# Tiles of four consecutive tokens per partition: a mixer's running sums by neighbour additions and one triangle product, one logit product a batch

## The chip, the cores and the metric

The kernel runs on one NeuronCore of a Trainium2 chip. The metric is the device time of one execution in microseconds (us). Engines are named as in the profile: PE is TensorE (PEld its weight loads), DVE VectorE, ACT ScalarE, POOL GpSimd, SP the engine that issues most DMAs (its queue is SPq).

## The reference, cut to what matters

Two layers on x of 8 batches x 512 tokens x 256 channels. Each layer adds to x a mixer's result times the Silu of a mixture of experts. Around the change, layer 0:

```python
xn = layernorm(x)
# mixer
q, k, v = split(rms_norm(xn) @ w_qkv.T); q = rms_norm(q); k = rms_norm(k)
w = exp(k); kv = w * v
w = cumsum(w, axis=tokens); kv = cumsum(kv, axis=tokens)
y = sigmoid(q) * kv / (w + 1e-06)
u, g = split(y @ w_swiglu.T); s = xn + (u * silu(g)) @ w_out.T
# experts: each of 16 experts takes its 64 best tokens of every batch
logits = silu(xn @ router_w1) @ router_w2
probs = softmax over tokens; weights, indices = top_k(probs, 64)
expert_out = (silu(xe @ w1) * (xe @ w2)) @ w3; f = scatter_add(weights * expert_out)
x = x + s * silu(f)
```

The running sum goes over all 512 tokens of a batch, for 512 channels (w and kv). Layer 1 has softmax attention with 16 heads and 8 experts of which each token takes 2, and a shared expert.

## The kernel before, in words

Everything is float32; the large expert products are split into a high and a low part and done as three products of the faster float32r form (`product3`, L93). A batch of 512 tokens is held as four tiles of 128 tokens: token 128 t + p stands in partition p of tile t (`tiled`, L1935). There are five stages, each a block with one instruction stream per engine and semaphores between them.

1. `layer0_norm` (L108): layernorm of the eight batches, transposition, router hidden layer (L162) and router logits: four small products per batch (L170), each copied by VectorE to `k.logits` (L247). SP loads x two batches ahead, then fills `f` with zeros (L141).
2. `layer0_mix_and_experts` (L261): first the choice of tokens (L708 to L746), for which four transposes (L428) bring the logits to one row per batch and expert; beside it batch 0's qkv products. Then batch 0's sums and divides, two qkv of batch 1, the first expert's input; then the main list.
3. `layer1_prepare` (L779): layernorms, projections and routing logits of layer 1.
4. `layer1_route` (L1097): slots of the chosen tokens.
5. `layer1_attend_and_feed` (L1216): attention beside the experts of layer 1, and the final sum.

**The order in stage 2** is a list written out by the program and walked by every engine. 16 experts have six steps each: ("up", e, 0..3), ("down", e, 0..1). The mixer's steps are ("qkv", n, t), ("sum", n, t), ("turn", n, 0), ("gates", n, 0..1), ("out", n, 0) for batch n and tile t. Before the change one mixer step follows each expert step, in one running list (L306 to L318); so a batch, 12 or 13 mixer steps, takes two experts. A step has its part on each engine:

- up (L406): 12 products of 512 columns into the banks GATE and VALUE, after `h_done` of the step before. ScalarE does the Silu (`expert_gate`, L505), VectorE the product with the value (`hidden`, L699), ScalarE its rounding (`high_h`, L510), VectorE the rest (`low_h`, L704). ScalarE rounds a weight of the next expert (`high_w`, L490) ahead of the Silu in up 1, 2, 3, and VectorE takes its rest (`low_w`, L688) between `hidden` and `low_h`.
- down (L415): 24 products of 256 columns; the first down waits for `h_lo` of each of the four parts. After it stands the transposition of the next expert's input (`transpose_x`, L398), then `high_x` (L499) and `low_x` (L693).
- qkv (L354): products of one tile into the banks QK and V, after `qkv_sb` of the tile before; VectorE copies them (`copy_qkv`, L635), ScalarE takes the sums of squares (`squared`, L461). After the fourth tile GpSimd makes the norm factors (`factors`, L559).
- exponentials (`exps`, L469, eight instructions) and the values (`keys_values`, L644) stand in the first down of an odd expert, and GpSimd's two partial sums (`partial`, L582) too.
- sum (L362): the tile's running sum by a product with an upper triangle of ones (L369) and, from tile 1 on, a product of ones with the sum of the tiles before (L372). VectorE then divides (`divide`, L652: four instructions, one of them a reciprocal of 1.75 us).
- turn (L375), gates (L382), out (L390): y transposed, its high part copied by ScalarE (`copy_y`, L479) and low part by VectorE (`low_y`, L669), the two gate products, `gate` (L485) and `gated` (L674), the last product and `residual` (L680).

Each engine does its parts strictly in the order of the list; an instruction that waits holds up all that stand behind it on its engine.

## Time and profile before

| | us |
|---|---|
| median of three runs | 1772.76 |
| lowest and highest run | 1771.67, 1774.93 |
| the profiled execution's own time | 1770.29 |
| its span, first to last instruction | 1768.3 |
| TensorE, VectorE, ScalarE, GpSimd busy | 1576.7, 1166.1, 918.9, 739.4 |
| mean granted TensorE clock | 0.942 of full |

By stage, read from the timelines: stages 1 and the choice of tokens to 99 us, experts and mixer of layer 0 to 605, the last scatter and the preparation of layer 1 to 772, routing to 802, attention and experts of layer 1 to the end.

How to read it: the profile is one execution. A timeline row is "start us, us, engine line op out<-in (partitions x elements) xcount [idle time before it <- what ended it]". Products overlap by a fraction of their length, so starts are compared, not ends. A granted clock of 1.00 is 2.4 GHz, 0.50 is 1.2 GHz.

### The profile page before, as it was taken

How to read it: one execution, taken by the hardware profiler on the slowest of the kernel's cores; microseconds unless marked ns; L12 is line 12 of the kernel's file. 1: busy time of each engine (PE TensorE's matmuls, PEld its weight loads, DVE VectorE, ACT ScalarE, POOL GpSimd, SP SyncE). 2: the span in 40 equal slices, each digit the busy share in tenths (PEclk: the TensorE clock that was granted, in tenths of full speed). 3: DMA queues.
4: the chain of work that ended last, by engine and by line, in shares of the span. 5: the costliest groups of instructions: out<-in, count | busy, mean ns of one | idle time of the engine just before them, and what ended most of it. 6: DMA issues, size and time to landing. Idle time of an engine off the chain costs nothing.

```text
span 1768.3 us, 27041 instructions
## 1 busy us (share of the span) xinstructions
PE 1576.7 (89%) x9562; PEld 1140.3 (64%) x9562; DVE 1166.1 (66%) x1847; ACT 918.9 (52%) x1426; POOL 739.4 (42%) x664
## 2 busy tenths in 40 slices
PE   6679999999999549954999999999999999999976
PEld 4357767877877435632677777777777777777631
DVE  6747567567557156656766666777777777777647
ACT  2335545545545123311555556777776777676644
POOL 3406335334433255502323223556565555555410
PEclk9899999999999869975999999999999999999975
DMA  6715546445333268845233335767676667666464
GB/s 223 232 37 114 149 96 141 122 99 141 74 90 87 24 214 293 308 161 150 87 107 114 100 124 137 196 159 195 165 188 161 182 165 185 175 176 184 115 187 147
DMA packets 218918, 265.38 MB, mean 150 GB/s; under 512 B 19616, under 2 KB 160416, under 8 KB 218784
## 3 DMA queue, kind: packets, MB, share of 16 engines
q1 hardware_dynamic: 191904, 227.92, 42.6%
q0 software_dynamic: 26880, 35.73, 11.3%
q8 instruction: 77, 1.26, 0.3%
q14 instruction: 57, 0.47, 0.1%
HBM read 174.30 MB, written 88.75 MB: 149 GB/s over the span
## 4 chain that ended last, share of the span: by engine, by line
PE 39%; SPq 4%; DVE 3%; DMA 2%; ACT 1%; issue 1%; POOL 0%; DVEq 0%; ACTq 0%
PE a_hidden_bank L93 16%; PE a_bank L93 8%; PE a_bank L1522 5%; PE a_max_bank L1491 5%; PE a_score_bank L1512 3%; DMA a_ka<-qk 2%; SPq L1314 2%; SPq L1318 2%; PE a_max_bank L1537 1%; PE a_bank L1529 1%; DVE a_w20lo L1828 1%; ACT a_xThi L1670 1%; DVE a_neg_max L1787 1%; DVE a_hT1lo L1818 0%; SPq L1380 0%
## 5 line engine op out<-in xcount | busy, mean ns | idle before, releaser
L1648 ACT ACTIVATE a_prob<-a_score_bank 128x1024 f32<-128x1024 f32 x240 | 246.2, 1026 | 257.1 <-PE a_score_bank L1512 214.9
L1787 DVE TENSOR_REDUCE a_neg_max<-a_max_bank 128x2 f32<-128x1024 f32 x249 | 304.1, 1221 | 91.8 <-PE a_max_bank L1491 86.2
L1444 POOL DMA_INDIRECT fs<-a_y,a_token x80 | 127.1, 1589 | 189.2 <-ACT a_y L1696 164.9
L1491 PE MATMUL a_max_bank<-a_ka,a_qa 48*128 48x512 f32 x498 | 128.0, 511 | 23.4 <-DVE a_neg_max L1787 12.0
L1522 PE MATMUL a_bank<-a_prob,a_va 128*32 128x512 f32 x1024 | 147.2, 650 | 0.5 <-DVE a_ml L1796 0.5
L602 POOL DMA_INDIRECT f<-e_ye,c_slot_row x64 | 100.7, 1573 | 84.6 <-issue 64.6
L1810 DVE SCALAR_TENSOR_TENSOR a_tg<-a_tg,a_hidden_bank 128x512 f32<-128x512 f32 x112 | 76.7, 685 | 82.1 <-ACT a_tg L1658 82.1
L1512 PE MATMUL a_score_bank<-a_qa,a_ka 50*128 50x512 f32 x480 | 100.2, 413 | 5.1 <-DMA a_qa<-a_ml 2.7
L702 DVE TENSOR_TENSOR e_h<-e_bank,e_sge 128x512 f32<-128x512 f32 x64 | 44.3, 691 | 89.2 <-ACT e_sge L508 82.6
L358 PE MATMUL e_bank<-m_wqkv,x_rows 128*128 128x512 f32 (+1 forms) x256 | 91.3, 501 | 8.8 <-DVE e_qkv L642 8.8
L1491 PEld LDWEIGHTS a_max_bank<-a_ka,a_qa 48*128 48x128 f32 x498 | 47.9, 189 | 69.9 <-DVE a_neg_max L1787 23.3
L93 PE MATMUL a_hidden_bank<-a_xThi,a_w31hi 128*128 128x256 f32 x288 | 89.4, 310 | 0.0
L93 PE MATMUL e_bank<-e_w3hi,e_heThi 128*128 128x256 f32 x256 | 80.1, 313 | 8.8 <-DVE e_heTlo L706 8.8
L1658 ACT ACTIVATE a_tg<-a_hidden_bank 128x512 f32<-128x512 f32 x112 | 67.2, 600 | 38.7 <-PE a_hidden_bank L93 37.2
L1814 DVE TENSOR_TENSOR a_h<-a_hidden_bank,a_tg 128x512 f32<-128x512 f32 x112 | 77.5, 692 | 13.8 <-PE a_hidden_bank L93 1.9
L93 PE MATMUL a_hidden_bank<-a_xThi,a_w11hi 128*128 128x256 f32 x288 | 85.2, 296 | 0.0
L93 PE MATMUL a_hidden_bank<-a_xThi,a_w31lo 128*128 128x256 f32 x288 | 82.3, 286 | 0.0
L93 PE MATMUL a_hidden_bank<-a_xTlo,a_w11hi 128*128 128x256 f32 x288 | 82.3, 286 | 0.0
L93 PE MATMUL a_hidden_bank<-a_xTlo,a_w31hi 128*128 128x256 f32 x288 | 82.1, 285 | 0.0
L93 PE MATMUL a_hidden_bank<-a_xThi,a_w11lo 128*128 128x256 f32 x288 | 82.1, 285 | 0.0
L508 ACT ACTIVATE e_sge<-e_bank 128x512 f32<-128x512 f32 x64 | 38.1, 595 | 81.1 <-PE e_bank L93 81.1
L595 POOL DMA_INDIRECT e_xg<-xn,c_slot_row x64 | 70.9, 1108 | 20.7 <-issue 18.6
(352 smaller groups left out, 4782.0 us busy)
## 6 DMA issues: line engine op xcount, KB each, us to landing
a_raw<-in_W SPq DMA_DIRECT2D x120, 512.0 KB
e_raw<-in_w SPq DMA_DIRECT2D x48, 512.0 KB, 3.8
a_qa<-qk SPq DMA_DIRECT2D x192, 64.0 KB
a_ka<-qk SPq DMA_DIRECT2D x192, 64.0 KB
xs<-c_pad SPq DMA_DIRECT2D x20, 516.0 KB
a_xg<-xs SPq DMA_DIRECT2D x20, 516.0 KB, 4.7
qk<-p_hi SPq DMA_DIRECT2D x32, 256.0 KB, 5.8
qk<-p_lo SPq DMA_DIRECT2D x32, 256.0 KB, 5.4
```

Of the source, the lines that this page charges most:

```text
L93: ins = nc.tensor.matmul(out, a[i][x], b[l][y], start=first and n == m == 0, stop=last and n == len(pairs) - 1 and m == 2)
L358: ins = nc.tensor.matmul(bank[:, 0:f1 - f0], m.xnT[:, n, ch, t * P:(t + 1) * P], m.wqkv[:, ch, f0:f1], start=ch == 0, stop=ch == DC - 1)
L595: nc.gpsimd.indirect_dma_start(xg[u][:, t, :], None, xn_rows, bass.IndirectOffsetOnAxis(k.slot_row[:, e, t:t + 1], 0)).then_inc(xg_in[u], 16)
L602: nc.gpsimd.indirect_dma_start(f_rows, bass.IndirectOffsetOnAxis(k.slot_row[:, e, t:t + 1], 0), ye[:, t, :], None, compute_op=ALU.add).the ...
L1444: nc.gpsimd.indirect_dma_start(f_rows, bass.IndirectOffsetOnAxis(token[x % 4][:, t:t + 1], 0), y[:, t, :], None, compute_op=ALU.add).then_ ...
L1491: nc.tensor.matmul(max_bank(g, m)[:, s, :], qa[q][rows, p, t * P:(t + 1) * P], ka[q][rows, p, :], start=True, stop=True).then_inc(p1_ps, 1)
L1512: nc.tensor.matmul(score_bank(g, u)[:, s, :], ka[q][rows, p, j * P:(j + 1) * P], qa[q][rows, p, :], start=True, stop=True).then_inc(s_ps, 1)
L1522: ins = nc.tensor.matmul(OB[rows, :], va[g % NR][:, j, rows], prob[j % 2][:, h_, :], start=j == 0, stop=j == T - 1, tile_position=(0, 32 * ...
L1648: nc.scalar.activation(prob[j % 2][:, 2 * p:2 * p + 2, :], score_bank(g, u)[:], ACT.Exp, scale=float(D) ** -0.5).then_inc(p_done, 1)
L1787: nc.vector.tensor_reduce(neg_max[:, g % 2, :, T * p + t], max_bank(g, m)[:], AX.X, ALU.max, negate=True).then_inc(mx_done, 1)
L1810: nc.vector.scalar_tensor_tensor(tg[:], tg[:], 1.0, GATE[:], ALU.add, ALU.mult).then_inc(act_done, 1)
L1814: nc.vector.tensor_tensor(h[:], VALUE[:], tg[:], ALU.mult).then_inc(h_done, 1)
```

## The change

- A tile is now four consecutive tokens per partition: token 4 p + t stands in partition p of tile t, and a DMA of a batch reads 4 KB in a row. `grouped` keeps the old form for the expert groups of layer 1.
- The running sum within a partition is three additions on GpSimd, tile t-1 onto tile t (`prefix`). One product of a strict triangle with the last tile gives what stands before each partition; `divide` adds it to numerator and denominator.
- The router's logits of all batches are gathered in one bank, one product of 512 columns a batch, with router_w2 set in zeros so that each batch writes its own 16 rows; one copy at the end instead of eight, and no transposes in the choice.
- The order of stage 2 is written per expert: in an even expert a qkv step after each up, in an odd one turn, gates, gates and out. Divides, exponentials, values and additions stand at new places. Batch 0's divides move from before the first expert into it, and batch 1's first two qkv steps as well.
- The zeros of `f` are written in stage 2, x is loaded four batches ahead, norm factors are made per batch.
- In stage 5 the loads of q and k are issued before two weight loads, and ScalarE rounds x before those weights.

The diff, cut to its core:

```diff
@@ layer0_norm, TensorE @@
 def logits(n):
-    for t in range(T):
-        ins = nc.tensor.matmul(B[6 + n % 2][:, t * E0:(t + 1) * E0], hT[:, n % 2, t * P:(t + 1) * P], rw2[:], start=True, stop=True)
+    first = (NB - 1 - n) * E0
+    nc.tensor.matmul(B[6][:], rw2[:, first:first + P], hT[:, n % 2, :], start=n == 0, stop=n == NB - 1).then_inc(lg_ps, 1)
...
+    order = []
+    for e in range(E0):
+        n, steps = e // 2 + 1, [("turn", e // 2, 0), ("gates", e // 2, 0), ("gates", e // 2, 1), ("out", e // 2, 0)]
+        for f in range(FC):
+            order.append(("up", e, f))
+            if e % 2:
+                order.append(steps[f])
+            elif n < NB:
+                order.append(("qkv", n, f))
+        order += [("down", e, 0), ("down", e, 1)]
+    def next_batch(e):
+        return (e + 1) // 2 if e % 2 and e + 1 < E0 else 0
...
-            def sum_(n, t):
...
+            def sum_(n):
+                pe.wait_ge(sums_done, 3 * (n + 1))
+                pe.wait_ge(s0_done, n)
+                nc.tensor.matmul(MIX[0][:], k.strict[:], wkv[:, T - 1, :], start=True, stop=True).then_inc(cum_ps, 1)
...
@@ TensorE, before the list @@
             transpose_x(0)
+            sum_(0)
...
                     down(a, i)
+                    if i == 0 and next_batch(a):
+                        sum_(next_batch(a))
                     if i == 0 and a + 1 < E0:
                         transpose_x(a + 1)
...
@@ ScalarE, the list @@
                     expert_gate(a, i)
                     high_h(a, i)
+                    if i == 0 and next_batch(a):
+                        exps(next_batch(a))
                 elif kind == "down":
-                    if i == 0 and a % 2 and a + 1 < E0:
-                        exps((a + 1) // 2)
...
@@ GpSimd @@
+            def prefix(n):
+                for t in range(1, T):
+                    pool.wait_ge(kv_done, T * n + t + 1)
+                    pool.wait_ge(sums_done, 3 * n + t - 1)
+                    nc.gpsimd.tensor_tensor(wkv[:, t, :], wkv[:, t - 1, :], wkv[:, t, :], ALU.add).then_inc(sums_done, 1)
...
+                elif kind == "up" and i == 1 and next_batch(a):
+                    prefix(next_batch(a))
...
@@ VectorE @@
             def divide(n, t):
+                total = MIX[0]
+                dve.wait_ge(cum_ps, n + 1)
                 dve.wait_ge(exp_done, 2 * T * n + T + t + 1)
+                own.step(nc.vector.scalar_tensor_tensor(den[:, t % 2, :], total[:, 0:D], CUM_EPS, wkv[:, t, 0:D], ALU.add, ALU.add))
+                own.step(nc.vector.tensor_tensor(y[:, t, :], total[:, D:2 * D], wkv[:, t, D:2 * D], ALU.add))
+                own.wait(1)
+                own.step(nc.vector.scalar_tensor_tensor(rec[:, t % 2, :], qkv[:, t, 0:D], 1.0, den[:, t % 2, :], ALU.add, ALU.mult))
                 own.wait()
                 own.step(nc.vector.reciprocal(den[:, t % 2, :], rec[:, t % 2, :]))
                 own.wait()
+                nc.vector.tensor_tensor(y[:, t, :], y[:, t, :], den[:, t % 2, :], ALU.mult).then_inc(y_done, 1)
...
@@ VectorE, the list @@
                     low_h(a, i)
+                    if a == 0:
+                        divide(0, i)
+                    elif a % 2 == 0 and i < 2:
+                        divide(a // 2, 2 + i)
+                    if i == 1 and next_batch(a):
+                        keys_values(next_batch(a))
+                elif kind == "down":
+                    if next_batch(a):
+                        divide(next_batch(a), i)
+                    if i == 0 and a + 1 < E0:
                         low_x(a + 1)
...
@@ layer1_attend_and_feed, SP @@
             load_x(0)
+            load_qk(0)
             load_w(0, 0)
             load_w(1, 0)
-            load_qk(0)
...
@@ layer1_attend_and_feed, ScalarE @@
+            high_x(0)
             high_w(0, 0)
             high_w(1, 0)
-            high_x(0)
...
     def tiled(ap, t=T):
-        return ap.rearrange("(b t p) d -> b p t d", t=t, p=P)
+        return ap.rearrange("(b p t) d -> b p t d", t=t, p=P)
```

## Rows read from the trace of the kernel before

**Rows 1.** Windows: us; busy (count) of PE, PEld, DVE, ACT, POOL; clock; DMA:

```profile
100.00:600.00 500.00, 474.05 (x2310) 369.35 (x2309) 305.68 (x445) 244.79 (x474) 196.72 (x179) 1.00 0.43 102
```

**Rows 2.** TensorE's waits in stage 2: total us, times, longest:

```profile
PE e_bank L93 <- DVE e_h L702: 10.4, 16, 1.4
PE e_bank L93 <- DVE e_heTlo L706: 7.0, 7, 2.1
```

**Rows 3.** TensorE's timeline: the same sum product, five batches apart:

```profile
233.70 1.02 PE L369 MATMUL e_bank<-e_wkv,c_upper 128*128 128x512 f32 x2
...
554.02 1.02 PE L369 MATMUL e_bank<-e_wkv,c_upper 128*128 128x512 f32 x2
```

**Rows 4.** TensorE's timeline through an even expert:

```profile
235.98 0.50 PE L93 MATMUL e_bank<-e_xeThi,e_w10hi 128*128 128x512 f32 x1 [0.41 <-DVE e_h L702]
...
238.83 2.74 PE L358 MATMUL e_bank<-m_wqkv,x_rows 128*128 128x512 f32 x8
241.48 0.50 PE L93 MATMUL e_bank<-e_xeThi,e_w10hi 128*128 128x512 f32 x1
...
248.97 0.39 PE L93 MATMUL e_bank<-e_w3hi,e_heThi 128*128 128x256 f32 x1 [0.83 <-DVE e_heTlo L706]
...
250.87 1.04 PE L403 MATMUL e_bank<-c_ident,e_xg 128*128 128x128 f32 x8
```

**Rows 5.** VectorE's timeline in the same expert:

```profile
232.08 0.42 DVE L657 SCALAR_TENSOR_TENSOR e_den<-e_bank,e_qkv 128x256 f32<-128x256 f32 x1
...
235.24 0.69 DVE L702 TENSOR_TENSOR e_h<-e_bank,e_sge 128x512 f32<-128x512 f32 x1
...
240.74 0.69 DVE L702 TENSOR_TENSOR e_h<-e_bank,e_sge 128x512 f32<-128x512 f32 x1
...
243.08 0.68 DVE L641 COPY e_qkv<-e_bank 128x512 f32<-128x512 f32 x1
...
246.49 0.69 DVE L702 TENSOR_TENSOR e_h<-e_bank,e_sge 128x512 f32<-128x512 f32 x1 [2.40 <-ACT e_sge L508]
```

**Rows 6.** ScalarE's timeline between the last two of rows 5:

```profile
244.13 0.42 ACT L467 ACTIVATE e_squares<-e_qkv 128x256 f32<-128x256 f32 x1 [2.03 <-DVE e_qkv L642]
...
244.94 1.04 ACT L497 ACTIVATE e_w21hi<-e_raw 128x1024 fp32r<-128x1024 f32 x1
```

**Rows 7.** ScalarE's timeline: the exponentials of a batch begin:

```profile
280.09 1.28 ACT L475 ACT_TABLE_LOAD   x1
281.38 1.71 ACT L475 ACTIVATE e_wkv<-e_qkv,e_scale 128x256 f32<-128x256 f32 x4
```

**Rows 8.** ScalarE and VectorE: high and low part of turned y:

```profile
264.63 1.07 ACT L483 ACTIVATE e_yThi<-e_bank 128x512 fp32r<-128x512 f32 x2
...
265.37 1.28 DVE L672 TENSOR_TENSOR e_yTlo<-e_bank,e_yThi 128x512 fp32r<-128x512 f32 x2
```

**Rows 9.** Expert 0's last fetch and first product, expert 15's last result:

```profile
84.59 0.95 POOL L595 DMA_INDIRECT e_xg<-xn,c_slot_row  x1 [0.30 <-issue]
...
99.32 0.47 PE L93 MATMUL e_bank<-e_xeThi,e_w10hi 128*128 128x512 f32 x1
...
604.42 0.84 ACT L521 ACTIVATE e_ye<-e_bank,c_slot_share 128x256 f32<-128x256 f32 x2 [2.04 <-PE e_bank L93]
```

**Rows 10.** GpSimd's timeline: first scatter and last fetch of an expert step:

```profile
226.56 1.62 POOL L602 DMA_INDIRECT f<-e_ye,c_slot_row  x1 [3.53 <-issue]
...
238.18 0.95 POOL L595 DMA_INDIRECT e_xg<-xn,c_slot_row  x1 [0.30 <-issue]
```

**Rows 11.** SP's and TensorE's timelines at the start of stage 5:

```profile
802.72 2.58 SPq L1341 DMA_DIRECT2D a_raw<-in_Ws  x2
...
816.66 0.80 PE L1491 MATMUL a_hidden_bank<-a_ka,a_qa 48*128 48x512 f32 x2 [7.19 <-DMA a_ka<-qk]
```

**Rows 12.** Windows of 2 us before expert 0, columns as in rows 1:

```profile
74.00:76.00 2.00, 0.00 (x0) 0.00 (x0) 1.97 (x6) 0.91 (x4) 0.57 (x3) 0.90 0.63 175
76.00:78.00 2.00, 0.14 (x1) 0.14 (x2) 1.64 (x8) 0.00 (x0) 1.72 (x3) 0.50 1.09 369
...
94.00:96.00 2.00, 0.13 (x2) 0.00 (x0) 1.83 (x3) 0.00 (x0) 0.00 (x0) 1.00 0.09 35
```

More of the change, by code:

```diff
@@ L198, in _ @@
-            own.step(nc.gpsimd.memset(m.half[:], -0.5))
-            own.wait()
+            flat_rstd = rstd[:].rearrange("p b t -> p (b t)")
+            flat_var = mv[:, :, :, 1].rearrange("p b t -> p (b t)")
+            first = Steps(pool, half_set, 2, 0)
+            first.step(nc.gpsimd.memset(m.half[:], -0.5))
+            first.step(nc.gpsimd.memset(rw2[:], 0.0))
+            first.wait()
+            first.end()
             for n in range(NB):
+                own = Steps(pool, r_done, 6, n)
+                now = slice(n * T, (n + 1) * T)
@@ L210, in _ @@
[L210 to L219 removed]
+                pool.wait_ge(rstd_done, n + 1)
@@ L221, in _ @@
+                own.wait()
+                own.step(nc.gpsimd.tensor_tensor(m.r2sq[:, now], m.r2[:, now], m.r2[:, now], ALU.mult))
+                own.step(nc.gpsimd.tensor_scalar(m.r2neg[:, now], m.r2[:, now], -1.0, None, ALU.mult))
+                own.wait()
+                own.end()
         @block.vector
@@ L748, in _ @@
             keys_values(0)
-            for t in range(T):
-                divide(0, t)
-            copy_qkv(1, 0)
             low_x(0)
-            copy_qkv(1, 1)
             for kind, a, i in order:
@@ L756, in _ @@
                     copy_qkv(a, i)
-                elif kind == "sum":
-                    divide(a, i)
                 elif kind == "turn":
```

172 lines of the change are left out of this document (52 added, 120 removed).

## The prediction

> **What bounds the kernel now.** The page's busy times stand first: TensorE leads. That is an average over five stages, and the change touches mostly the second, mixer and experts of layer 0. So next came the table of windows for that stage: of 500 us TensorE is busy 474, VectorE 306, ScalarE 245, at full clock [rows 1]. TensorE's waits in it are small: the largest sum is 10.4 us, before up products, in 480 us [rows 2]. TensorE bounds this stage, and what is taken off it is worth its full time, as long as the other engines still deliver. Whether they do can't be read from busy shares; it hangs on the order of each engine's queue. For that I read the timelines of TensorE, VectorE and ScalarE through one batch, that is, two experts.
>
> Two readings carry everything. One batch takes (554.02 - 233.70)/5 = 64.1 us [rows 3]. And there is a loop between VectorE and ScalarE: where a step holds a copy of q, k, v, the expert product `hidden` starts at 240.74 and the next at 246.49, 5.75 us later, although an up and a qkv product take TensorE only 2.85 + 2.65 = 5.5 us [rows 4, 5]. The reason: the copy starts at 243.08, the squares on ScalarE wait for it (244.13), the weight rounding stands behind the squares (244.94), the Silu behind that, and `hidden` behind the Silu [rows 5, 6]. From the start of the copy to the next `hidden` it is 3.4 us; from `hidden` to the copy 2.3 with a weight split between, 2.0 without (an estimate: the 1.2 us split overlaps ScalarE's 0.65 us copy).
>
> **The change, part by part.** (a) Products. Seven products with the triangle and the ones become one per batch. A qkv step is 1536 columns in 2.65 us [rows 4], so 512 columns are 0.88 us; six fewer are 5.3 us a batch, 37 us in the seven batches that lie in this stage. This is the whole gain of a reader who counts TensorE alone. The additions move to GpSimd, three a batch; they are done some 9 us before the triangle product is wanted (the last rival).
>
> (b) Divides in even experts. A divide takes 3.16 us now (232.08 to 235.24) [rows 5] and has one more 0.42 us instruction, of which 0.34 shows: 3.5 us. The old order had sums and qkv in different steps. The new one puts divides 2 and 3 of the batch behind `low_h` of up 0 and up 1 of the even expert, and the copy of qkv of the same step behind them. So the divide lies inside the loop: intervals of `hidden` are 2.0+3.5+3.4 = 8.9, 2.3+3.5+3.4 = 9.25 and then 5.75. With the first `hidden` 3.8 us after the expert's start (up product and Silu) the fourth starts at 27.7. The down product resumes 2.5 us after it (246.49 to 248.97), its last 16 products take 1.9 (to 250.87), transposes 0.9, second down product 24 x 0.12 = 2.9 [rows 4]: 35.9 us for an even expert. TensorE's own work in it is 29 us, so 7 us are waits: 1.9 and 3.4 before the second and third qkv, the rest shorter.
>
> (c) Exponentials in odd experts. They move from the down product to behind up 0. ScalarE then loads the Exp table (1.28) and runs eight exponentials (1.6 + 1.6) [rows 7], from 5.1 to 9.65 us of the expert. Behind them stand the copy of turned y and, through VectorE, its low part, 2.0 us from the copy's start to the end (264.63 to 266.65) [rows 8]. The gates product starts at 11.7, where TensorE was ready at 7.4: 4.3 us of wait. Then the weight rounding (1.0), the way back to the Silu table (1.28) and the Silu put the second `hidden` at 13.5, and the values (1.7 us, four instructions) behind it delay the first gated product to 18.2, the second gates product to 18.3 (ready 17.15). Out ends at 27.2, down at 30.2, the triangle product at 31.1, transposes 32.0, second down 34.9. VectorE can start divide 0 only at 31.2 and has the next expert's low x behind it: 31.2+3.5+1.3 = 36.0. An odd expert takes 36.1.
>
> (d) The ends. Expert 0 has a divide in all four steps: intervals 8.0, 8.9, 9.25, and a fourth divide and copy before its low x: 39.6 us. Expert 14 has divides without qkv: 28. Expert 15 has the mixer's last steps and neither: 28.
>
> Stage: 39.6 + 7x36.1 + 6x35.9 + 28 + 28 = 563.7 us. Now it is 99.3 to 604.4, 505.1 [rows 9]. **+58.6 us.** Bounds: if every interval came out as cheap as today's, -37; if TensorE also slows in the gaps, +70 (below).
>
> (e) The way to expert 0. Batch 0's sums, divides and the copies of batch 1 leave it. The last fetch of expert 0 ends at 85.5 today [rows 9]. With 2 us less ahead of it (the tail of the norm stage loses four transposes and eight small copies and gains one 0.6 us copy; 0 to 4), 1.7 for landing, 2.0 for transposes at the low clock, 1.9 for high and low x: 89.3, against 99.3. Less 1.5 for products that still run at the low clock: -8.5, between -4 and -12. The router's wider product is one of 512 columns for four small ones: nothing. GpSimd's factors per batch are covered by a batch period of 3.7 us there; if that cover is gone, up to 2 us.
>
> (f) Layer 1. The loads of q and k go ahead of two weight loads whose issue takes 2.6 us (802.72) [rows 11], and the first maximum waits for k, 7.2 us [rows 11]: -2.6, between 0 and -3. What they are moved past, the weights, is wanted only 15 us later.
>
> (g) Tiles of four tokens per partition turn pieces of 1 KB into 4 KB. Where DMA doesn't end a wait this is worth nothing; at the very end the loads of x1 and fs do: -1.5 (0 to -4).
>
> (h) The clock. The granted clock stayed at 1.00 through 2 us with 0.13 busy; where two such windows stand in a row, 4 us with 0.14 busy, it is 0.90 in the first and 0.50 in the second [rows 12]. The gap of (c) is 4.3 us. At half speed the gates product takes 2.7 more, and 1.6 of that reaches the second gates product: 7 x 1.6 = 11 at most, 0 at least; the gap is as long as the one that fell, but its clock fell only within it, so a part of the gaps may pass: I take 5.
> The Trainium skill, "TensorE: Matmul & The Clock Gate", section "HAM oscillation — how this bites in real kernels", says that a wait inside a loop makes every turn of it start at the low clock again. By that the term would be the 11, not 5; the rows of the 4 us gap agree, no row shows a gap inside a loop.
>
> Sum: 58.6 - 8.5 - 2.6 - 1.5 + 5 = +51. The profiled execution took 1770.3 us (span 1768.3), so 1821.3; the median of the runs shown lies 2.5 above it, 1823.8. I say 1823.
>
> **The rivals.** *TensorE's saving counts.* Place: the step of up and qkv in even experts. If the divide and the exponentials fit into idle time (VectorE is idle 194 of 500 us [rows 1]), a batch takes 64.1 - 5.3 = 58.8 and the total is 1772.8 - 37 - 8.5 - 2.6 - 1.5 = 1723. It decides at the interval of `hidden`: below 5.5 us TensorE stays the bound. For it speaks the idle time; against it the 5.75 us loop seen today with no divide in it. Chance 0.10.
>
> *Half the stalls.* The odd experts hide theirs, because TensorE has gates and out products to put between; then these cost about 30.5 and the total is 1823 - 7x5.6 = 1784. For: the waits there are only partly in series. Against: the gates product itself is what waits. Chance 0.10.
>
> *The clock falls in every gap*, those of 3.4 us in even experts too. Each such fall makes a qkv product take 2.65 more, of which about 1 is not covered by the loop: 6x1 + 11 instead of 5: 1835. Chance 0.20. It is the skill's rule named in (h) at its full price.
>
> *The change doesn't do what it says*: the triangle product needs the whole batch's additions first, which GpSimd does behind eight indirect transfers; it would then be late and the wait in front of it would replace the products. GpSimd's transfers take 12.6 us (226.56 to 239.13) [rows 10] from about 1 us into the odd expert, the values are there at 16.7, the additions end at 20.7, and the product is due at 30.2. Late only if GpSimd lags 9 us: 10 us a batch, 1890. Chance 0.03.
>
> My forecast 0.57.
>
> **How the numbers follow.** A difference of 0.2%, 3.5 us, is about what a measurement of this kernel can tell from none. Faster: the first rival, 0.10, and 0.02 of the second's lower edge. Same: 0.03. Slower: the rest, 0.85. The forecast's own range is 1805 to 1840 (terms e to h at their ends, and 1 us an expert on the loops). To hold 8 in 10 it must take in the clock case and most of the second rival's upper half: 1790 to 1845.
>
> **What would show it.** In the changed profile: `hidden` in even experts 9 us apart twice, then under 6; ScalarE's squares released by VectorE's copy, late; TensorE's waits before qkv products near 2 and 3.4 us, before the gates product near 4; a batch of 72 us; TensorE busy some 410 us in 500. The prediction is wrong if the batch period is under 62, and its step (c) alone if no wait over 2 us stands before gates. The way to expert 0 is right if its first up product starts near 90.

## The result, and the profile after

The changed kernel took 1821.28 us (median of four runs, 1819.79 to 1823.27) against 1772.22 us for the kernel before: ratio 1.0275, 95% interval 1.0257 to 1.0293. Predicted were 1823 and a range of 1790 to 1845. The profiled execution has a span of 1821.6 us against 1768.3, so 53.3 us more; the medians differ by 49.1, because the profiled execution of the kernel before was shorter than its median (1770.29) and that of the changed kernel the slowest of its four. The table lays the 53.3 out along the program; all times are read from timelines as in [rows 9, 11].

| mark | before | after | difference of the stretch | predicted |
|---|---|---|---|---|
| first up product of expert 0 | 99.32 | 96.41 | -2.9 | -8.5 |
| first GpSimd instruction of stage 3 | 619.12 | 681.34 | +65.1 | +63.6 |
| first load of stage 5 | 802.29 | 864.13 | -0.4 | 0 |
| end of the span | 1768.3 | 1821.6 | -8.5 | -4.1 |

The same window as [rows 1], for the changed kernel (us; busy of PE, PEld, DVE, ACT, POOL; clock; DMA), and TensorE's largest waits between 100 and 650 us:

```profile
100.00:600.00 500.00, 421.79 (x1955) 325.61 (x1954) 302.03 (x442) 221.14 (x441) 183.87 (x174) 0.94 0.39 95
```

```profile
PE e_bank L93 <- issue: 37.1, 15, 4.1
PE e_bank L356 <- DVE e_qkv L623: 33.6, 15, 3.1
PE e_bank L93 <- DVE e_h L682: 11.3, 18, 2.3
```

TensorE is busy 52 us less of 500, and the stage is longer. The prediction had said 410 us busy; it is 422, part of it at the low clock (the mean granted clock is 0.94). Two waits have come that [rows 2] do not have: before the first gates products (4.1 us each, in the first line) and before qkv products (up to 3.1 us). The triangle product shows the batch period, (604.10 - 167.43)/6 = 72.8 us against 64.1 [rows 3]:

```profile
167.43 1.02 PE L363 MATMUL e_bank<-e_wkv,c_strict 128*128 128x512 f32 x2
...
604.10 1.02 PE L363 MATMUL e_bank<-e_wkv,c_strict 128*128 128x512 f32 x2
```

**An even expert.** VectorE's timeline, and ScalarE's at the second copy; these rows answer to [rows 5, 6]:

```profile
394.80 0.69 DVE L682 TENSOR_TENSOR e_h<-e_bank,e_sge 128x512 f32<-128x512 f32 x1 [0.56 <-ACT e_sge L491]
...
400.16 0.69 DVE L622 COPY e_qkv<-e_bank 128x512 f32<-128x512 f32 x1
...
403.58 0.69 DVE L682 TENSOR_TENSOR e_h<-e_bank,e_sge 128x512 f32<-128x512 f32 x1 [2.40 <-issue]
...
412.70 0.69 DVE L682 TENSOR_TENSOR e_h<-e_bank,e_sge 128x512 f32<-128x512 f32 x1 [2.40 <-ACT e_sge L491]
...
418.46 0.69 DVE L682 TENSOR_TENSOR e_h<-e_bank,e_sge 128x512 f32<-128x512 f32 x1 [2.40 <-ACT e_sge L491]
```

```profile
401.21 0.42 ACT L451 ACTIVATE e_squares<-e_qkv 128x256 f32<-128x256 f32 x1 [5.06 <-DVE e_qkv L623]
```

One `hidden` follows the other after 8.78, 9.12 and 5.76 us. The copy starts at 400.16, the instant divide 2 (396.79 to 400.12) has ended, and ScalarE's squares had waited 5.06 us for it. TensorE waits for VectorE's copies before two of its qkv products, 1.83 and 3.02 us.

**An odd expert.** ScalarE, then TensorE and VectorE; these answer to [rows 7, 8]:

```profile
431.63 1.28 ACT L458 ACT_TABLE_LOAD   x1
432.93 1.71 ACT L458 ACTIVATE e_wkv<-e_qkv,e_scale 128x256 f32<-128x256 f32 x4
...
436.13 1.05 ACT L466 ACTIVATE e_yThi<-e_bank 128x512 fp32r<-128x512 f32 x2
...
438.15 1.28 ACT L491 ACT_TABLE_LOAD   x1
439.45 0.60 ACT L491 ACTIVATE e_sge<-e_bank 128x512 f32<-128x512 f32 x1
```

```profile
438.13 0.47 PE L93 MATMUL e_bank<-e_yThi,e_wswhi 128*128 128x512 f32 x1 [4.11 <-issue]
...
442.56 0.39 PE L93 MATMUL e_bank<-e_xeThi,e_w11hi 128*128 128x512 f32 x1
...
445.88 0.47 PE L93 MATMUL e_bank<-e_yThi,e_wswhi 128*128 128x512 f32 x1 [0.44 <-DVE e_guT L658]
```

```profile
430.26 0.69 DVE L682 TENSOR_TENSOR e_h<-e_bank,e_sge 128x512 f32<-128x512 f32 x1 [4.33 <-ACT e_sge L491]
...
440.08 0.69 DVE L682 TENSOR_TENSOR e_h<-e_bank,e_sge 128x512 f32<-128x512 f32 x1 [2.05 <-ACT e_sge L491]
...
442.42 2.71 DVE L628 SCALAR_TENSOR_TENSOR e_wkv<-e_qkv,m_r,e_wkv 128x256 f32<-128x256 f32 x4
445.05 0.68 DVE L658 TENSOR_TENSOR e_guT<-e_bank,e_sg 128x512 f32<-128x512 f32 x1
446.11 0.69 DVE L682 TENSOR_TENSOR e_h<-e_bank,e_sge 128x512 f32<-128x512 f32 x1 [0.38 <-ACT e_sge L491]
```

From 431.63 to 439.45 ScalarE is between two Silus: one table load, eight exponentials, the copy of y, a weight, the other table load. The first gates product starts at 438.13 after 4.11 us of waiting (TensorE's up products had ended at 434.02); the second `hidden` comes 9.82 us after the first. One row is new: the four values take 2.71 us; in the kernel before the same four took 1.67. The granted clock in that gap, and after it (columns as above):

```profile
434.00:438.00 4.00, 0.03 (x1) 0.00 (x0) 1.26 (x2) 4.00 (x9) 3.08 (x4) 1.00 0.61 73
439.00:442.00 3.00, 3.00 (x8) 2.32 (x7) 1.92 (x3) 1.67 (x3) 1.71 (x2) 0.50 0.38 104
```

Here it stays at 1.00 through the idle 4 us and is 0.50 from 439 to 442, while TensorE is fully busy. That isn't so in each batch: in four of the seven gaps before gates the clock fell inside the gap, 0.2 to 2.0 us before its end, and in two of these it stayed low for 6.9 us instead of 3.5.

### The profile page after: what moved, and what is told of

It reads as the page before. It is cut to its first block, busy times and chain, and to the rows that moved or that the text cites. A ratio compares the mean times of both kernels' runs of the same rounds, so it can differ in the third digit from the quotient of the medians.

```text
span 1821.6 us, 26824 instructions
## 1 busy us (share of the span) xinstructions
PE 1562.7 (86%) x9414; PEld 1132.4 (62%) x9414; DVE 1185.3 (65%) x1871; ACT 921.4 (51%) x1427; POOL 755.0 (41%) x714
## 4 chain that ended last, share of the span: by engine, by line
PE 36%; SPq 4%; DVE 4%; DMA 3%; ACT 2%; issue 1%; POOL 0%; DVEq 0%; ACTq 0%
PE a_hidden_bank L93 15%; PE a_bank L93 7%; PE a_bank L1500 5%; PE a_max_bank L1469 4%; PE a_score_bank L1490 2%; DMA a_ka<-qk 2%; SPq L1292 2%; SPq L1296 2%; PE a_max_bank L1515 1%; DVE a_w20lo L1806 1%; DVE a_neg_max L1765 1%; PE a_bank L1507 1%; ACT a_xThi L1648 1%; DMA a_qa<-a_ml 0%; DVE a_raw L1813 0%
## 5 line engine op out<-in xcount | busy, mean ns | idle before, releaser
L356 PE MATMUL e_bank<-m_wqkv,x_rows 128*128 128x512 f32 (+1 forms) x256 | 105.6, 562 | 41.6 <-DVE e_qkv L623 40.3
L356 PEld LDWEIGHTS e_bank<-m_wqkv,x_rows 128*128 128x128 f32 x256 | 53.4, 215 | 92.0 <-DVE e_qkv L623 47.9
L451 ACT ACTIVATE e_squares<-e_qkv 128x256 f32<-128x256 f32 x64 | 26.1, 409 | 119.9 <-DVE e_qkv L623 119.9
```

The source lines that it names most:

```text
L356: ins = nc.tensor.matmul(bank[:, 0:f1 - f0], m.xnT[:, n, ch, t * P:(t + 1) * P], m.wqkv[:, ch, f0:f1], start=ch == 0, stop=ch == DC - 1)
```

## The experiments

Each result is a ratio to the kernel before, run on the same chip; the changed kernel stands at 1.0275, and 0.001 is 1.8 us. The intervals are about 0.002 to either side, so a difference of two ratios is good to some 4 to 5 us. For anything smaller, the intervals between the starts of `hidden` in the profile are read. Those of even experts and the first one of odd experts repeat within 0.1 us from batch to batch, with one exception that is named below; the last two of an odd expert trade with each other (5.88 to 7.25 and 5.44 to 6.28 us), and their sum is read. One more measure is the time from one transposition of an expert's input to the next (`transpose_x`, in the down steps); it cuts the same batch at other places than `hidden` does, so its values for odd and even experts are other ones. Stage 5 must be kept apart: in the eleven profiles below that have the changed kernel's stage 5, it took anything from 956.2 to 963.4 us.

### 1. Copy ahead of divide

```diff
                 if kind == "qkv":
                     copy_qkv(a, i)
+                    if 2 <= a and i < 2:
+                        divide(a - 1, 2 + i)
...
-                    elif a % 2 == 0 and i < 2:
+                    elif a == E0 - 2 and i < 2:
                         divide(a // 2, 2 + i)
```

> The changed kernel, with VectorE's copy of qkv ahead of divides 2 and 3 in even experts 2 to 12. Theory (the divide lies inside the VectorE-ScalarE loop): low h ends 2.0 us after hidden, copy 1.1 and divide 3.5 follow, so hidden intervals of 8.78 and 9.12 us become 6.65 and 7.0, the third stays 5.76; ScalarE's squares no longer wait 5 us for the copy, TensorE's waits before qkv products vanish. 4.25 us in each of 6 experts: 25 us less than the changed kernel, about 1796. Rival one (the slow clock of TensorE behind the 3 us gaps is what costs): the same removal also brings full-speed qkv products, about 1 us more an expert, 1790. Rival two (something else than the copy's place sets the even expert, the weights or the down product): under 5 us in all.

Measured: 1789.64 us, ratio 1.0121 (1.0099 to 1.0142), 27 us under the changed kernel. VectorE in expert 4 (its `hidden` of up 1 to up 3; the one of up 0 is at 242.67):

```profile
248.96 0.69 DVE L682 TENSOR_TENSOR e_h<-e_bank,e_sge 128x512 f32<-128x512 f32 x1
...
255.59 0.69 DVE L682 TENSOR_TENSOR e_h<-e_bank,e_sge 128x512 f32<-128x512 f32 x1
...
261.35 0.69 DVE L682 TENSOR_TENSOR e_h<-e_bank,e_sge 128x512 f32<-128x512 f32 x1 [2.40 <-ACT e_sge L491]
```

Intervals of 6.29, 6.63 and 5.76, together 5.0 us less than before the edit; expected were 4.25. The 0.7 us between lie in the two intervals that hold a divide: VectorE goes from `low_h` through copy and divide to the next `hidden` without a wait, and its instructions overlap by more than the sum had allowed. They are not the slow clock of rival one, although the total is its 1790: from the last `hidden` of an even expert to the first of the next it is 11.7 us here and 11.8 in the changed kernel. The order of two VectorE operations is worth 5 us an expert; step (b) is shown.

### 2. Exponentials behind the turn

```diff
                 elif kind == "turn":
                     copy_y(a)
+                    if a + 1 < NB:
+                        exps(a + 1)
...
-                    if i == 0 and next_batch(a):
-                        exps(next_batch(a))
```

> The changed kernel, with ScalarE's exponentials behind the copy of turned y instead of ahead of it. The wait of 4.1 us before the gates product goes, but the second Silu still stands behind the exponentials and both table loads. Theory (the second hidden is what counts, the gates product's wait only shows it): the idle time moves to the third up product, about 4 us, with its own clock fall; hidden intervals in odd experts stay 9.8 and 6, the total within 5 us of the changed kernel. Rival (the wait before gates is itself the loss): up to 4.1 us in each of 7 experts, 29 us less.

Measured: 1821.99 us, ratio 1.0296 (1.0279 to 1.0313): no gain. TensorE's wait has moved from the gates product to the third up product and is as long as before, and `hidden` keeps its 9.84 us:

```profile
439.83 0.79 PE L93 MATMUL e_bank<-e_xeThi,e_w11hi 128*128 128x512 f32 x1 [4.11 <-DVE e_h L682]
```

```profile
429.24 0.69 DVE L682 TENSOR_TENSOR e_h<-e_bank,e_sge 128x512 f32<-128x512 f32 x1 [4.33 <-ACT e_sge L491]
...
439.08 0.69 DVE L682 TENSOR_TENSOR e_h<-e_bank,e_sge 128x512 f32<-128x512 f32 x1 [6.56 <-ACT e_sge L491]
...
445.68 0.69 DVE L682 TENSOR_TENSOR e_h<-e_bank,e_sge 128x512 f32<-128x512 f32 x1 [0.97 <-ACT e_sge L491]
```

The largest wait in TensorE's list was not itself the loss; it only showed that the second `hidden` was late.

### 3. No table loads

This kernel takes squares where exponentials belong, so it computes another function; the eight instructions take as long as before (1.69 and 1.69 us for two times four, against 1.71 and 1.69).

```diff
+                func = ACT.Square if n else ACT.Exp
...
-    nc.scalar.activation(wkv[:, t, 0:D], qkv[:, t, D:2 * D], ACT.Exp, ...
+    nc.scalar.activation(wkv[:, t, 0:D], qkv[:, t, D:2 * D], func, ...
```

> The changed kernel, with Square in place of Exp for the running sums of batches 1 to 7, so that this part of the result is another function; it needs no change of ScalarE's table. Theory (ScalarE's block of 5.9 us between two Silus is the price in odd experts, 2.56 of it table loads): the second hidden comes 2.5 us earlier, and the gap before gates shrinks from 4.1 to 2.9 us. If the clock then stays up, 3.0 us in each of 7 odd experts, 21 less, 1800; if it still falls in the gap, 1.3 each, 9 less. Rival (the odd experts are held by VectorE's values, gated and low w beside GpSimd's additions): under 5 us in all.

Measured: 1805.74 us, ratio 1.0204 (1.0187 to 1.0221), 13 us less, between the two expected values (21 and 9). The second `hidden` comes 6.97 us after the first, 2.85 earlier, and the gap before gates is 2.7 us; behind it the clock stayed up in five of seven experts. Only 2.2 of the 2.85 reach the end of the expert (33.45 against 35.68 us from one transposition of x to the next), because the next limit is near: the values now take 3.31 us, and the second gates product waits 1.19 for the gated product that VectorE makes behind them.

```profile
425.31 0.69 DVE L683 TENSOR_TENSOR e_h<-e_bank,e_sge 128x512 f32<-128x512 f32 x1 [0.62 <-ACT e_sge L492]
...
427.65 3.31 DVE L629 SCALAR_TENSOR_TENSOR e_wkv<-e_qkv,m_r,e_wkv 128x256 f32<-128x256 f32 x4
430.88 0.68 DVE L659 TENSOR_TENSOR e_guT<-e_bank,e_sg 128x512 f32<-128x512 f32 x1
```

### 4. The clock, and what lay beside it

Two edits: 14 products that nobody reads, in TensorE's gap before gates, and GpSimd's additions held back until all values are there.

```diff
+    FILL = 14
...
             def gates(n, j):
+                if j == 0:
+                    pe.wait_ge(qkv_sb, T * min(n + 2, NB))
+                    for r in range(FILL):
+                        nc.tensor.matmul(QK[:], w1[1][0][:, 0, 0:P], xeT[0][:, 0, :], start=True, stop=True)
...
             def prefix(n):
+                pool.wait_ge(kv_done, T * (n + 1))
                 for t in range(1, T):
```

The first edit alone:

> The changed kernel, with 14 products of 512 columns (3.2 us, into an idle bank, read by nobody) on TensorE ahead of the first gates product of each batch, so that TensorE is busy through most of its 4.1 us wait. Theory (the wait makes the granted clock fall and that costs 1.6 us in each of 7 odd experts): the gates product runs at full clock, 2.75 instead of 4.4 us, the third hidden comes 4.4 instead of 6.0 us after the second, 11 us less than the changed kernel. Rival (the slow gates product is covered by other waits): no change. If the products delay the gates product: up to 2 us an expert more.

Measured: 1831.50 us, ratio 1.0339 (1.0317 to 1.0361), 11 us more. The clock did stay up (window behind the filling, columns as above; the filling leaves 0.9 us of the gap):

```profile
436.00:440.00 4.00, 3.22 (x14) 2.67 (x15) 1.96 (x4) 3.21 (x5) 2.87 (x3) 1.00 0.40 105
```

but the third `hidden` came after 5.54 us instead of 6.0 and the fourth after 6.58 instead of 6.2: odd experts 35.65 us against 35.68, from transposition to transposition. The slow clock costs nothing there; the second gates product now waits 1.99 us for the gated product, which stands behind the values. In expert 15 the filling costs 3 us. The rest of the 11 this profile doesn't have (it is the fastest of the five runs, and its span is 3.7 us above the changed kernel's). So the second edit alone, both together, and the first without the last batch:

> The changed kernel, with GpSimd's first addition waiting for all four values of VectorE instead of two. Theory (the values take 2.71 us instead of 1.67 because GpSimd's additions run beside them, and that delays the first gated product): the values take 1.7 us again; the second gates product no longer waits 0.4 us, and nothing more is won, since the slow clock of the first gates product keeps the third up product late: 0.4 us in each of 7 odd experts, 3 less than the changed kernel. Rival (the clock is not in this place): 1 us each, 7 less. Rival two (the additions are not what slows the values): values stay at 2.7 us, no change.

> The changed kernel, with both: additions wait for all values, and the 14 idle-bank products ahead of the first gates product of batches 0 to 6 (not of the last). Theory (slow clock and late values stand side by side, each covers the other, so that filling alone won nothing): now the second gates product comes 1.0 us earlier, hidden intervals 9.82, 5.54 and about 5.5; 1 us in each of 7 odd experts, 7 less than the changed kernel. Rival (something third holds the second gates product): no change.

> The changed kernel, with the 14 idle-bank products ahead of the first gates product of batches 0 to 6 alone. Theory: the earlier kernel with this edit was slower only by what the products of the last batch cost in expert 15 (3 us); without them it equals the changed kernel within 2 us, as the odd experts of its profile did (35.65 against 35.68 us). Rival (the idle-bank products cost time outside these gaps too, for instance by a lower clock elsewhere): still 8 to 11 us over the changed kernel.

Measured: additions waiting 1814.34 us, ratio 1.0247 (1.0230 to 1.0263), 5 less; both 1818.69 us, 1.0260 (1.0236 to 1.0284), 3 less; filled alone 1826.88 us, 1.0314 (1.0295 to 1.0333), 7 more. VectorE's values and gated product in the kernel with both:

```profile
437.06 1.67 DVE L634 SCALAR_TENSOR_TENSOR e_wkv<-e_qkv,m_r,e_wkv 128x256 f32<-128x256 f32 x4
438.64 0.68 DVE L664 TENSOR_TENSOR e_guT<-e_bank,e_sg 128x512 f32<-128x512 f32 x1
```

The values take 1.67 us as soon as no addition runs beside them. Odd experts: 34.97 us with that edit, 34.62 with both, 35.65 with the filling alone, 35.68 with neither. So the late values cost 0.7 us by themselves, where 0.4 was expected; the slow clock costs nothing by itself and 0.35 once the values are early: the late values had covered it. The filled kernels' medians are worse than these intervals say. For the kernel with both, the profile shows why: stage 2 is 10 us shorter than in the changed kernel, but stage 5, which the edits don't touch, took 963.4 us against 957.5. For the filled-alone kernel part of the cause is in its profile: there the 2.0 us gap that filling leaves before the second gates product made the clock fall in four of seven odd experts, and those took 37.2 us or more, not 35.66. The first row below is the gap, the second what follows 1 us behind it:

```profile
446.00:448.00 2.00, 0.16 (x1) 0.00 (x0) 2.00 (x3) 0.60 (x1) 1.85 (x2) 1.00 0.77 266
449.00:452.00 3.00, 3.00 (x9) 2.31 (x8) 2.40 (x2) 0.25 (x1) 1.85 (x1) 0.50 1.04 247
```

In the first filled kernel's profile the same gap never did that. That it is this which differs from run to run is my reading, not shown.

### 5. What the seven products were worth

On the kernel before, with the product of ones left out of batches 1 to 7 (the running sum then starts anew in each tile):

```diff
-                ins = nc.tensor.matmul(MIX[t % 2][:], k.upper[:], wkv[:, t, :], start=True, stop=t == 0)
-                if t:
+                ins = nc.tensor.matmul(MIX[t % 2][:], k.upper[:], wkv[:, t, :], start=True, stop=t == 0 or n > 0)
+                if t and n == 0:
```

> The kernel before, with the product of ones (the sums of the tiles before) left out of tiles 1 to 3 for batches 1 to 7: three of the seven products of a batch go, the running sum is then only within a tile. If what is taken off TensorE in this stage is worth its full time (the prediction's step a), 3 x 0.88 us in each of 7 batches: 18.5 less than before. Theory: these products filled time in which the up products wait for the Silu and VectorE's hidden anyway; in the two steps of the even expert (tiles 2 and 3) VectorE's divide, which ends just as the next hidden starts, sets the interval, so they are worth nothing, and at most the one of the second down step counts: 0 to 6 us less than before.

Measured: 1760.85 us, ratio 0.9948 (0.9929 to 0.9967), 9 us less, half of what TensorE was spared. In stage 2 the profile has 7 x 0.78 = 5.5: the batch goes from 64.10 to 63.32 us. VectorE, as in [rows 5]:

```profile
228.98 0.69 DVE L702 TENSOR_TENSOR e_h<-e_bank,e_sge 128x512 f32<-128x512 f32 x1
...
234.13 0.69 DVE L702 TENSOR_TENSOR e_h<-e_bank,e_sge 128x512 f32<-128x512 f32 x1
...
239.63 0.69 DVE L702 TENSOR_TENSOR e_h<-e_bank,e_sge 128x512 f32<-128x512 f32 x1
...
245.39 0.69 DVE L702 TENSOR_TENSOR e_h<-e_bank,e_sge 128x512 f32<-128x512 f32 x1 [2.40 <-ACT e_sge L508]
```

The intervals 5.15, 5.50 and 5.76 are those of the kernel before, to 0.01 us, though 1.77 us of products are gone from the first two steps: there the `hidden` follows the divide at once. Only the stretch over the down products became shorter, by 0.74. The median moved by more than the 0 to 6 us expected, and the interval (6 to 13 us) just misses the 5.5. The profile has the rest where nothing was changed: stage 5 took 960.4 us against 966.0. So this experiment's evidence is the 0.78 us a batch, not the total; and both are far from the 18.5 that step (a) would give.

### 6. The way to expert 0

```diff
+            sp.wait_ge(xg_in[0], 16 * ST)
             for c in range(NB):
                 sp.dma_start(at(f_b, c), k.pad[:, :, 0:D]).then_inc(m.zeroed, 16)
```

> The changed kernel, with the eight DMAs that write zeros into f issued only after the first expert's rows have landed. Theory (the rows of expert 0 come late because 4 MB of zeros are on the DMA queues): TensorE's 12 us wait ends near 89.5 instead of 92.4, the first up product stands near 93.5 instead of 96.4: 3 us less (1.5 to 4), about 1818. Rival (the landing takes 5 us whatever else moves, and the way to expert 0 is set by the later choice of tokens alone): no change, within 0.7 us at the first up product.

Measured: 1819.83 us, ratio 1.0277 (1.0258 to 1.0296); the total can't tell 3 us. The profile can: TensorE's wait for expert 0's rows ends at 89.45 instead of 92.39, the first up product stands at 93.47 (changed kernel 96.41, and 94.97 to 96.15 in the eight others with the zeros in place). So 1.5 to 2.9 us. The landing itself is clearer: from the end of the last fetch's issue to the transposition it is 4.98 us in the changed kernel and 2.6 to 4.9 in those eight, and 1.84 to 1.89 in the three kernels with the zeros later (this one, the next, and that of experiment 8).

The second half of that way is in ScalarE's timeline of stage 1, changed kernel, the router's Silu, and the same in the kernel that follows, which has the edit below and the zeros later as well:

```profile
25.88 1.12 ACT L192 ACTIVATE n_hT<-n_bank 128x512 f32<-128x512 f32 x1 [2.07 <-PE n_bank L164]
```

```profile
24.73 0.60 ACT L192 ACTIVATE n_hT<-n_bank 128x512 f32<-128x512 f32 x1 [2.07 <-PE n_bank L164]
```

```diff
-nc.scalar.activation(hT[:, n % 2, :].rearrange("h (p t) -> h t p", t=T), B[4 + n % 2][:].rearrange("h (t p) -> h t p", t=T), ACT.Silu)
+nc.scalar.activation(hT[:, n % 2, :], B[4 + n % 2][:], ACT.Silu)
```

> The changed kernel, with the zeros of f after expert 0's rows and the router's Silu in stage 1 reading and writing its 512 elements in their order (the logits then stand in another order of tokens, so other tokens are chosen; the work is the same). Theory (the way to expert 0 came out 5.6 us longer than predicted because of two terms not counted: the Silu that spreads its elements takes 1.11 instead of 0.60 us in the loop of each of 8 batches, and the zeros' DMAs delay expert 0's rows): the batch period of stage 1 goes from 4.1 back to 3.65 us, the maximum of the logits from 54.0 to about 51 us, and the first up product stands at 90.5 us, against 96.4 in the changed kernel and 93.5 with the zeros moved alone: 6 us less than the changed kernel. Rival (VectorE's or GpSimd's new work per batch sets the 4.1 us): the period stays 4.1, first up product at 93.5.

Measured: 1817.31 us, ratio 1.0250 (1.0230 to 1.0270), 4 less. The period of stage 1 is 3.65 us instead of 4.1, the maximum of the logits stands at 49.77 instead of 54.05, the first up product, 1.4 us earlier than expected, at

```profile
89.08 0.76 PE L93 MATMUL e_bank<-e_xeThi,e_w10hi 128*128 128x512 f32 x1
```

### 7. Stage 5's loads

```diff
             load_x(0)
-            load_qk(0)
             load_w(0, 0)
             load_w(1, 0)
+            load_qk(0)
...
-            high_x(0)
             high_w(0, 0)
             high_w(1, 0)
+            high_x(0)
```

> The changed kernel, with the old order at the start of stage 5 (two weight loads ahead of the loads of q and k, ScalarE rounds those weights before x). Theory (order of the loads is the gain there): stage 5's first maximum stands 5 us later again, from 9.1 to 14 us after the stage's start, and the total is 3 to 5 us over the changed kernel. Rival (the tiles' 4 KB pieces or the lighter queues made the 8.5 us that stage 5 is shorter): under 1.5 us over the changed kernel.

Measured: 1826.70 us, ratio 1.0308 (1.0286 to 1.0330), 6 us more. From the stage's first load to the first product with k it is 9.1 us in the changed kernel and 8.6 in that of experiment 8; with the old order it is 12.4 here, 14.4 before, and 11.8 in the kernel of experiment 5, whose stage 5 is that of before. So the order is worth 3 to 5 us at that place. The whole stage took 966.0, 963.5 and 960.4 us in the three profiles with the old order, and 956.2 to 963.4 in the eleven with the new one: the ranges overlap, so its length can't tell the order's worth. No run takes the 4 KB pieces alone, so what they are worth stays open; nothing above needs them.

### 8. The same products, other places

The changed kernel's arithmetic, with the parts of VectorE, ScalarE and GpSimd and the triangle product placed anew, and the zeros as in experiment 6. The core:

```diff
@@ TensorE: triangle product behind up 0 of the even expert @@
+                    if i == 0 and a % 2 == 0:
+                        sum_(a // 2)
@@ ScalarE, VectorE, GpSimd (no lines shown): exps, keys_values, prefix in ("down", 0) of the odd expert @@
@@ VectorE: divide keeps its first three instructions, the other two are @@
+            def invert(n, t):
+                dve.wait_ge(den_steps, 3 * (T * n + t + 1))
+                nc.vector.reciprocal(rec[:, t, :], rec[:, t, :]).then_inc(rec_steps, 1)
+                dve.wait_ge(rec_steps, T * n + t + 1)
+                nc.vector.tensor_tensor(y[:, t, :], y[:, t, :], rec[:, t, :], ALU.mult).then_inc(y_done, 1)
@@ VectorE, the list: divide 0 between hidden and low_h of up 0 @@
                     copy_qkv(a, i)
+                    if i + 1 < T:
+                        divide(a - 1, i + 1)
...
+                    if a % 2 == 0 and i == 0:
+                        invert(a // 2, 0)
+                        invert(a // 2, 1)
                     if i == 0 and a + 1 < E0:
                         low_x(a + 1)
+                    if a % 2 == 0 and i == 0:
+                        invert(a // 2, 2)
+                        invert(a // 2, 3)
```

> The changed kernel's arithmetic and TensorE order, with VectorE's and ScalarE's parts placed anew: exponentials, values and additions back in the first down step of the odd expert, the triangle product behind up 0 of the even expert, each divide cut in two (three instructions of 1.25 us between copies of qkv in the up steps; reciprocal and product, 2.2 us each, in the first down step), zeros of f after expert 0's rows. Theory (the change lost by where it put the divides and exponentials, not by its products): even experts 31, odd 29.5 us, batch 60.5 instead of 72.8, expert 0 4 us shorter: 1821 - 86 - 4 - 3 = 1728. Rival (VectorE, busy 29 of 31 us of the even expert, becomes the bound): hidden intervals of 6.5 us there, 1756. If it were the arithmetic itself (additions on GpSimd late, fifth instruction of the divide) that costs: over 1790.

Measured: 1722.99 us, ratio 0.9727 (0.9708 to 0.9747): 48 us faster than the kernel before and 98 faster than the changed one. VectorE in an even expert, and the window (columns as above):

```profile
278.91 0.69 DVE L684 TENSOR_TENSOR e_h<-e_bank,e_sge 128x512 f32<-128x512 f32 x1 [4.33 <-ACT e_sge L491]
...
285.14 0.69 DVE L684 TENSOR_TENSOR e_h<-e_bank,e_sge 128x512 f32<-128x512 f32 x1 [1.41 <-ACT e_sge L491]
...
290.91 0.69 DVE L684 TENSOR_TENSOR e_h<-e_bank,e_sge 128x512 f32<-128x512 f32 x1 [1.41 <-ACT e_sge L491]
...
296.67 0.69 DVE L684 TENSOR_TENSOR e_h<-e_bank,e_sge 128x512 f32<-128x512 f32 x1 [1.41 <-ACT e_sge L491]
```

```profile
100.00:550.00 450.00, 426.11 (x2171) 345.83 (x2171) 324.47 (x487) 239.26 (x472) 208.07 (x186) 1.00 0.53 125
```

Intervals 6.23, 5.77, 5.76; from transposition to transposition even experts take 29.5 and odd ones 30.0 us, a batch 59.45, where TensorE's own work was put at 58.8. TensorE is busy 426 of 450 us, and from expert 1 to expert 13 the clock never falls. Its largest wait left, 10 us in all, is for y before the turn. Of the 98 us, 97.8 lie in stage 2 of the profile (472.4 us against 570.2). Of the 48, 32.7 do; 4.5 are the earlier first up product, and 9 stand in stage 5. The edit moves several things at once, so it shows that the places cost the time and the arithmetic does not, but it doesn't divide the 98 us among them.

## Why the prediction was right, and where it was not

**The total** came out closer than its parts, and that is luck. In the profiles the forecast was +51 and the measured difference 53.3. The way to expert 0 cost 5.6 us more than forecast, stage 2 with (h) in it 1.5 more, and layer 1 came out 4.8 better, most of it in stage 5, which scatters by 7. The mechanism was right: the new places of divides and exponentials lengthen the way from one `hidden` to the next, and stage 2 alone is 65 us longer where 63.6 were forecast. The misses are below.

**(a), the worth of a product, was too simple.** "What is taken off it is worth its full time, as long as the other engines still deliver" held only with its second half, and in the kernel before they did not deliver in the steps where the products stood: experiment 5 gives 0 for the two products beside divides and 0.7 to 0.8 us for the one in the down step. Nearly all of the 37 us are there once the parts are well placed (experiment 8: stage 2 is 32.7 us shorter than before).

**(b) is right in mechanism and size**: 8.78, 9.12 and 5.76 us against 8.9, 9.25 and 5.75; even experts 35.46 us from first `hidden` to first `hidden` (394.80 to 430.26) against 35.9. That the first two are shorter than forecast comes mostly from the divide, which took 3.33 us (396.79 to 400.12) instead of 3.5. Experiment 1 shows the cause.

**(c) is right in mechanism, one term was missing.** Wait before gates 4.11 (4.3 predicted), second `hidden` 9.82 after the first (13.5 - 3.8 = 9.7). But the second gates product started at 19.2 us of the expert instead of 18.3, and the odd expert took 37.0 (430.26 to 467.30) instead of 36.1. The step that failed is "the values (1.7 us, four instructions)": beside GpSimd's additions they take 2.71, and held apart from them they take 1.67 and the odd expert 36.3 us (experiment 4). The prediction asked whether the additions are late, not what they do to VectorE. I had also named the waiting gates product as the argument against "half the stalls"; experiment 2 shows that this argument was the wrong one: the odd expert is long because its second `hidden` is late, wherever TensorE waits for it.

**(d)**: expert 0 39.4 us (39.6), expert 14 29.1 (28). Stage by these steps 563.7, measured 570.2 (96.41 to the last result at 666.63).

**(e) failed in size**: -2.9, outside its -4 to -12. "With 2 us less ahead of it" forgot the new layout's price in ScalarE's Silu, about 1.1 instead of 0.60 us in each of eight turns of the loop of stage 1, and "1.7 for landing" was five, because the step moved the zeros of `f` into that landing. With both undone the first up product stands at 89.08. The prediction had 89.3 on its way (its terms add up to 89.1) and 90.8 after the 1.5 us for the low clock.

**(f) and (g)**: -8.5 against -4.1 together. Experiment 7 gives the order 3 to 5 us at the first product with k, where (f) had 2.6; stage 5 itself scatters by 7, so the rest has no cause shown. No row stood behind the 1.5 us of (g), and no run shows them.

**(h) had the right sum for the wrong reason.** The clock fell at each of the seven gaps of 4.1 us, and once in each even expert from 2 to 12 too (at the 3.0 us gap in five of six, at the 1.8 us one in the sixth), which the third rival had priced at 1 us each. So that rival was near in the number of falls and wrong in their price. Filling the gap gave back nothing alone (experiment 4). In even experts the slow qkv product is covered by the loop of (b) in five of the six; in the sixth, where the clock stayed low twice as long, the last `hidden` came after 6.96 instead of 5.76 us, and the expert took 1.4 us more. With one odd expert that took 0.5 more (37.52 us, again with the long fall), about 2 us of this profile can be laid to the clock, where (h) had 5. The Trainium skill's rule, "TensorE: Matmul & The Clock Gate", "HAM oscillation — how this bites in real kernels", is right here in that the clock fell at each turn's 4.1 us gap; the 11 us that (h) gave for it at full price did not come. The seven odd experts together were 7.0 us longer than (c); 5 of these went with the late values (0.7 each, experiment 4), and that is what filled the place of (h).

The first rival (1723) said that TensorE stays the bound only with `hidden` under 5.5 us apart in even experts. Experiment 8 took 1723 without meeting that (6.23, 5.77 and 5.76 us): a batch came to 59.45 us all the same, so the interval of an even expert's up steps alone doesn't decide it. That both numbers are 1723 is chance: experiment 8 has less from stage 2 than the rival (32.7 against 37) and more from stage 5. The additions were never late, so that rival is out: experiment 8 has the same three, and TensorE's list of waits has none before the triangle product.

## What to carry to other kernels

Price a removed instruction by what stands beside it in the same step: if another engine's loop (here copy, squares, Silu, `hidden`) already fills the step, it is worth nothing, and what is put into that loop counts in full (here 5 us an expert for one order of two operations). The longest wait of the busiest engine tells where something is late, not what; move the suspected cost and see whether the wait goes or only moves. When work is put on an idle engine or in a new layout, count what it does to the durations of instructions that run beside it or read that layout.

## What the runs showed of the hardware

VectorE beside GpSimd: four instructions with two operands in SBUF took 1.67 us alone and 2.71 beside GpSimd's additions, a weight split 1.22 and 2.08. The gated product, with one operand in PSUM, took 0.68 in the same stretch (445.05). The loss is not spread over the four: the first took 0.48 us, and the whole 1.0 us falls on the one that ran beside the first addition. It ended 0.3 us after that addition, as if it had been held up until then:

```profile
442.42 0.48 DVE L628 SCALAR_TENSOR_TENSOR e_wkv<-e_qkv,m_r,e_wkv 128x256 f32<-128x256 f32 x1
443.62 1.51 DVE L628 SCALAR_TENSOR_TENSOR e_wkv<-e_qkv,m_r,e_wkv 128x256 f32<-128x256 f32 x1
443.38 1.46 POOL L567 TENSOR_TENSOR e_wkv<-e_wkv 128x512 f32<-128x512 f32 x1 [2.37 <-DVE e_wkv L628]
```

The Trainium skill, "SBUF — State Buffer", section "Who interferes with whom", says that a VectorE instruction with two SBUF inputs contends with a GpSimd instruction that reads SBUF; by that rule, the trace agrees.

A Silu of 512 elements that writes its output four elements apart took 1.07 to 1.13 us, against 0.60 in order.

Switching ScalarE's table took 1.28 us, and the next instruction started at once (431.63, 432.93). Without the two switches the second `hidden` was 2.85 us earlier, 1.4 each. The Trainium skill, "ScalarE: Activation LUTs", section "What ACT_TABLE_LOAD costs", adds a drain of about 1.38 us to each load; by it two switches would cost 5.3 us (an estimate), and the 2.85 measured here leave no room for that.

The granted clock fell 13 times from expert 1 to expert 13 of the changed kernel: seven times 0.1 to 1.0 us after TensorE had resumed work, as at 438.7 after a gap that ended at 438.13, and six times inside the gap. The length of a gap alone did not decide whether it fell: at 2.0 us it fell in four of seven odd experts of one profile and in none of another, at 2.7 us in two of seven, at 4.1 us in all seven.
